# One-core graph attention kernel: peeling bits with fewer dependent VectorE steps, capping empty slots while own scores are added, and a reordered ending with more spare matmuls

## What is computed

```
h = x @ W
e = (h @ a1)[:, None] + (h @ a2)[None, :]
e = where(e > 0, e, 0.2 * e)
e = where(adj > 0, e, -9e15)
y = x + elu(softmax(e, axis=1) @ h)
out = (y - mean(y)) / sqrt(var(y) + 1e-5)
```

## Time and profile before

| | us |
|---|---|
| three timed runs | 715.48, 714.63, 712.79 (median 714.63) |
| the profiled execution, its own time | 716.63 |
| its span, first to last instruction | 714.8 |
| share of the span in which PE, DVE, ACT, POOL were busy | 78%, 67%, 73%, 63% |
| mean granted clock of PE, as a share of full speed | 0.874 |

### The profile page before, as it was taken

The page is one execution under the profiler, slowest core; times in us unless marked ns, Lnnn a source line. Parts: engine busy times, 40 slices in busy tenths (PEclk is TensorE's granted clock), DMA queues, the critical chain, the costliest instruction groups (busy, mean ns, idle before and its releaser), DMA issues.

```text
span 714.8 us, 11813 instructions
## 1 busy us (share of the span) xinstructions
PE 558.3 (78%) x3025; PEld 352.9 (49%) x3074; DVE 479.6 (67%) x2059; ACT 521.6 (73%) x416; POOL 447.1 (63%) x676
## 2 busy tenths in 40 slices
PE   0867887776979787777788778887787988887985
PEld 0323455453546554544555555554455555545564
DVE  2375577776585867677666667677666577675774
ACT  0847778787877887878788777878787788787601
POOL 2015367767575776677666766767667577677771
PEclk9979999988887989999999988899999688888976
DMA  9999999999999999999999999999999999999362
GB/s 352 328 416 429 426 424 426 426 423 425 425 427 429 426 426 428 427 427 426 427 425 427 431 425 426 428 427 427 428 426 428 431 425 426 426 427 423 128 182 73
DMA packets 34598, 285.57 MB, mean 399 GB/s; under 512 B 5528, under 2 KB 13872, under 8 KB 18064
## 3 DMA queue, kind: packets, MB, share of 16 engines
q1 hardware_dynamic: 29024, 276.83, 92.7%
q0 software_dynamic: 5120, 8.42, 3.3%
q10 hardware_dynamic: 432, 0.07, 0.1%
HBM read 283.18 MB, written 4.19 MB: 402 GB/s over the span
## 4 chain that ended last, share of the span: by engine, by line
DMA 64%; PE 16%; ACT 11%; issue 4%; DVE 2%; POOL 1%; SPq 1%; ACTq 0%; POOLq 0%; DVEq 0%
DMA adj_sb<-in_adj 62%; ACT adj_squared L603 10%; PE fold L718 8%; DMA a_sb<-in_L_gnn_a 2%; PE x_att_ps L771 1%; PE misc L748 1%; PE fold L714 1%; PE fold L830 1%; PE small L733 1%; PE small L757 1%; POOL edge_row L375 1%; SPq L413 1%; PE x_att_ps L774 0%; PE h_ps L798 0%; PE fold L785 0%
## 5 line engine op out<-in xcount | busy, mean ns | idle before, releaser
L603 ACT ACTIVATE adj_squared<-adj_sb 128x4096 bf16<-128x4096 int32 x128 | 462.5, 3614 | 105.6 <-DMA adj_sb<-in_adj 99.7
L718 PE MATMUL fold<-adj_sb,bit_ident 128*128 128x512 bf16 x993 | 302.9, 449 | 10.2 <-DMA adj_sb<-in_adj 4.8
L528 POOL DMA_INDIRECT nb<-in_x,index x160 | 165.9, 1037 | 90.3 <-issue 59.8
L718 PEld LDWEIGHTS fold<-adj_sb,bit_ident 128*128 128x128 bf16 x1024 | 110.8, 108 | 154.2 <-issue 68.1
L953 DVE MAX8 top_map<-fold 128x8 f32<-128x512 f32 x128 | 89.3, 699 | 70.7 <-PE fold L718 57.0
L714 PE MATMUL fold<-col_no,ident_bf 128*128 128x512 bf16 x112 | 47.8, 426 | 104.9 <-DMA adj_sb<-in_adj 90.9
L375 POOL TENSOR_SCALAR edge_row<-row_iota,edge_in 128x128 f32<-128x128 int32 x186 | 128.9, 707 | 0.0
L393 POOL TENSOR_TENSOR spread<-edge_row,edge_w 128x384 f32<-128x384 f32 x60 | 55.0, 935 | 74.6 <-DVE edge_w L1079 74.6
L508 POOL TENSOR_SCALAR empty_diag<-ident,counts 128x128 f32<-128x128 f32 x64 | 39.5, 623 | 64.3 <-DVE counts L989 33.5
L714 PEld LDWEIGHTS fold<-col_no,ident_bf 128*128 128x128 bf16 x128 | 16.4, 128 | 125.0 <-issue 86.8
L771 PEld LDWEIGHTS x_att_ps<-spread,nb 128*128 128x128 f32 x372 | 57.5, 221 | 8.0 <-issue 4.1
(11 more groups left out here) (139 smaller groups left out, 631.2 us busy)
## 6 DMA issues: line engine op xcount, KB each, us to landing
adj_sb<-in_adj SPq DMA_DIRECT2D x127, 2048.0 KB, 14.8
out<-x_sb SPq DMA_DIRECT2D x2, 1536.0 KB
nb<-in_x,index POOLq DMA_INDIRECT x160, 2.4
adj_sb<-in_adj SPq DMA_DIRECT2D x2, 1024.0 KB, 17.0
out<-x_sb SPq DMA_DIRECT2D x4, 128.0 KB
out<-x_sb SPq DMA_DIRECT2D x1, 384.0 KB
out<-x_sb SPq DMA_DIRECT2D x2, 64.0 KB
W_sb<-in_L_gnn_W ACTq DMA_DIRECT2D x1, 64.0 KB, 7.8
```

The source lines that it names most:

```text
L528: nc.gpsimd.indirect_dma_start(out=nb_of(j, g)[:, c, :], out_offset=None, in_=x[:, :], in_offset=bass.IndirectOffsetOnAxis(ap=index[:, g, ...
L603: nc.scalar.activation(adj_squared[:, h % 2, :], adj_sb[:, h % LOAD_SLOTS, :], ACT.Square, accum_out=half_sum[:, h:h + 1]).then_inc(square ...
L718: last = nc.tensor.matmul(fold[:, h % LOAD_SLOTS, :], bit_ident[:, b, :], adj_low[:, h % LOAD_SLOTS, b * FOLD:(b + 1) * FOLD, 0], start=Fa ...
```

## The change

Three things are edited.

**Peeling.** Before, `lists` took the codes apart one after another: subtract the column, mask the exponent (the leading bit), subtract it, mask the exponent again. Now a scaled copy of the numbers, larger by 2^8, is made first (`peel[:, 0, :]`), so that the leading bit can be masked with the column still in place, and the two masks that give `lead` are one instruction of twice the width, which keeps only the low bits of the exponent. There are eight instructions before the first `max` as before; seven of them were followed by a wait for their own end, now five are. A constant is set once at the start.

**Cap.** `scores` applied `cap` by an instruction of its own after the leaky slope. Now the row's own part is added and the cap applied in one instruction for each tile (two of 128 x 10), and the separate one (128 x 20) is gone.

**Ending.** On ACT `copy_sums(back2)` comes ahead of `exp_weights(back1)`. On PE two calls of `keep_warm` grow from 4 and 5 to 8 and 8 matmuls, and a `keep_warm(2)` is added behind `send_scores(final)`.

```diff
-    FIRST_EXP = 127 + 9
+    LIFT = 2.0 ** 8
+    KEPT_BITS = 0b00010111 << 23
+    FIRST_EXP = 16
     COL_0 = FOLD * (FIRST_EXP + BITS - 1) + HALF
-    NO_CODE = COL_0 - N - FOLD
+    NO_CODE = COL_0 - N
...
-                copy_sums(*back2)
                 exp_elu(*back2)
...
                 exp_elu(*back3)
+                copy_sums(*back2)
                 exp_weights(*back1)
...
-                keep_warm(4)
+                keep_warm(8)
                 send_shares(*back1)
-                keep_warm(5)
+                keep_warm(8)
                 send_scores(*final)
+                keep_warm(2)
                 sum_neighbours(*back1)
...
-                    v.after(nc.vector.tensor_scalar(top_int[:], top_map[:].rearrange("p q s -> p (q s)"),
-                                                    1.0 / UNIT, float(FOLD // 2), ALU.mult, ALU.add))
+                    maps = top_map[:].rearrange("p q s -> p (q s)")
+                    nc.vector.tensor_scalar(peel[:, 0, :], maps, LIFT / UNIT, LIFT * (FOLD // 2), ALU.mult, ALU.add)
+                    v.after(nc.vector.tensor_scalar(top_int[:], maps, 1.0 / UNIT, float(FOLD // 2), ALU.mult, ALU.add))
+                    nc.vector.tensor_tensor(top_lead[:], peel[:, 0, :].bitcast(i32),
+                                            exp_bits[:, 0:1].to_broadcast(flat), ALU.bitwise_and)
                     v.after(nc.vector.tensor_tensor(top_col[:], top_int[:], col_bits[:, 0:1].to_broadcast(flat),
                                                     ALU.bitwise_and))
-                    nc.vector.tensor_tensor(from_base[:], half_base[:].rearrange("p q s -> p (q s)"), top_col[:],
-                                            ALU.subtract)
-                    v.after(nc.vector.tensor_tensor(top_code[:], top_int[:], top_col[:], ALU.subtract))
-                    v.after(nc.vector.tensor_tensor(lead[:, 0, :], top_code[:].bitcast(i32),
-                                                    exp_bits[:, 0:1].to_broadcast(flat), ALU.bitwise_and))
-                    v.after(nc.vector.tensor_tensor(rest_code[:], top_code[:], lead[:, 0, :].bitcast(fp32),
+                    nc.vector.tensor_tensor(peel[:, 1, :], peel[:, 0, :], top_lead[:].bitcast(fp32), ALU.subtract)
+                    v.after(nc.vector.tensor_tensor(from_base[:], half_base[:].rearrange("p q s -> p (q s)"), top_col[:],
                                                     ALU.subtract))
-                    v.after(nc.vector.tensor_tensor(lead[:, 1, :], rest_code[:].bitcast(i32),
-                                                    exp_bits[:, 0:1].to_broadcast(flat), ALU.bitwise_and))
+                    v.after(nc.vector.tensor_tensor(
+                        lead[:].rearrange("p k s -> p (k s)"), peel[:].rearrange("p k s -> p (k s)").bitcast(i32),
+                        kept_bits[:, 0:1].to_broadcast([P, PEELS * 2 * PAIR * 8]), ALU.bitwise_and))
...
-                    mine = s_all[:, bass.ds(j * BODY + g * PAIR, PAIR)]
-                    v.after(nc.vector.tensor_tensor(score[:], t_row_ps, mine.unsqueeze(2).to_broadcast(slots),
-                                                    ALU.add))
+                    for t in range(PAIR):
+                        last = nc.vector.scalar_tensor_tensor(
+                            score[:, t, :], t_row_ps[:, t, :], s_all[:, bass.ds(j * BODY + g * PAIR + t, 1)],
+                            cap[:, g, t, :], ALU.add, ALU.min)
+                    v.after(last)
                     v.after(nc.vector.scalar_tensor_tensor(score_l[:], score[:], ALPHA, score[:],
                                                            ALU.mult, ALU.max))
-                    v.after(nc.vector.tensor_tensor(score_l[:], score_l[:], cap[:, g, :, :], ALU.min))
```

More of the change, by code:

```diff
@@ L120, in graph_attention @@
         exp_bits = sb("exp_bits", [P, 1], i32)
+        kept_bits = sb("kept_bits", [P, 1], i32)
         half_base = sb("half_base", [P, 2 * PAIR, 8], i32)
@@ L149, in graph_attention @@
         top_col = sb("top_col", [P, 2 * PAIR * 8], i32)
-        top_code = sb("top_code", [P, 2 * PAIR * 8], fp32)
-        rest_code = sb("rest_code", [P, 2 * PAIR * 8], fp32)
+        peel = sb("peel", [P, PEELS, 2 * PAIR * 8], fp32)
+        top_lead = sb("top_lead", [P, 2 * PAIR * 8], i32)
         from_base = sb("from_base", [P, 2 * PAIR * 8], fp32)
@@ L911, in _ @@
                 nc.vector.memset(exp_bits[:], EXP_BITS)
+                nc.vector.memset(kept_bits[:], KEPT_BITS)
                 nc.vector.memset(col_bits[:], FOLD - 1)
```

## The result

| | before | after |
|---|---|---|
| median of 9 timed runs, us | 715.28 (711.57 to 719.98) | 720.06 (718.39 to 722.79) |
| ratio after / before | | 1.0071, 95% interval 1.0046 to 1.0097 |
| the profiled execution, its own time | 716.63 | 722.79 |
| its span | 714.8 | 721.0 |
| last packet of adjacency ends (DMA records) | 670.2 | 679.3 |

The change costs 4.8 us by the medians: it is slower where faster was forecast, and 720.06 lies above the predicted range of 707.7 to 712.5. The last two lines say where, for the two profiled executions: the loop lost 9.1 us, and what follows it won back 2.9.

What follows compares the result with a forecast made beforehand. DMA bounds the loop to 664 us, then a PE, DVE, ACT, POOL chain, with PE at half clock. Gains of 4.9 and 0.95 make 5.85: 710.8 from the profile, 708.8 from the median; 709.6 taken, range 707.7 to 712.5.

Steps and rivals of the forecast that it cites:

- the loop to 664 unchanged: Loop, 60 to 664 us: DMA covers peeling and cap, so both are worth nothing there; without cover 8 us.
- a constant more at the start: Start of the kernel: the new constant's instruction lies behind the first transfers, so no cost was counted.
- the 5.85 us of all the others: Ending: 4.9 us to the final shares plus 0.95 us of DVE idle time, for an execution like the profiled one.
- the 0.06 for a slower kernel: Whole kernel: chance 0.06 that it is slower by 3.6 us.
- the half-clock products: Ending, PE: clock already down at `times_W(back2)`, nine more products cost 3.9 us on the path; 716.7 us, chance 0.06.
- The sum: Whole change: 5.85 us off the profiled 716.63 gives 710.8; 709.6 was taken as the forecast.
- The 4.9 us to the end of `send_shares(final)`: Ending, PE: at full clock the final shares are done at 696.7 instead of 701.61, 4.9 us sooner.
- the term of 0.95: Ending, DVE: its idle 0.96 us before the final group's first tile goes, worth 0.95 us.
- The first rival: Ending: timed runs lose less to the clock than the profiled one, leaving 3.85 us; 710.8 us, chance 0.22.
- The later fall: Ending, PE: the clock still falls, at about 693, and 3.2 of 5.85 us are gone; 712.0 us, chance 0.14.
- the gather: Ending, DVE: gathered rows land late for the final `t_slot`, up to 2.5 us of gain go; 711.3 us, chance 0.08.
- the small edits only: Ending: the reorder does not remove PE's idle time, only DVE's 0.25 us remain; 714.4 us, chance 0.05.

Runs made afterwards that it cites:

- e1: The changed kernel with 352 unused bytes ahead of `nb`, so that it starts at a multiple of 512 again; 710.96 us, ratio 0.9935.
- e3: The kernel before with the edits of the ending alone, `nb` where it was; 710.22 us, ratio 0.9930.
- e5: The kernel before with `nb` alone 32 bytes off its multiple of 512; 722.10 us, ratio 1.0089.
- e10: The kernel before with `nb` alone 256 bytes off its multiple of 512; 714.44 us, ratio 1.0005.
- e9: The kernel before with `nb` alone 128 bytes off its multiple of 512; 725.79 us, ratio 1.0123.
- e6: The kernel before with `nb` alone 64 bytes off its multiple of 512; 723.82 us, ratio 1.0102.

## Why the prediction was wrong

**The step that failed** is the one that put the loop at nothing: "the loop to 664 unchanged", and before it "In the loop both are worth nothing, since DMA covers them". The reading was right, the loop is bound by DMA and nothing computed in it can shorten it. The conclusion was not, for an edit can also change the DMA. The prediction knew of "a constant more at the start" and priced it by its instruction, which "lies behind the first transfers". Its 32 bytes, and the 128 of the wider temporaries, cost 9.1 us by pushing `nb` off a multiple of 256: the term that was put at nothing is larger than the 5.85 us of all the others. None of the rivals had it, and the 0.06 for a slower kernel rested on the half-clock products or on "a wait that I don't see". Where one resource is at a share of 1.01 for 600 us, 1.4% more time on each of its packets (615.4 to 624.1 ns) is worth more than the whole change to the ending.

With `nb` placed back the rest can be judged:

- **The sum.** Predicted 709.6 for the whole change; e1 has 710.96. Its profiled execution took 709.25, where the sum had 710.8 for one like the profile before; 1.2 of the 1.55 us between are luck, for its final `pick` ended 2.3 us behind the last packet and not 3.5 (see the last point of this list).
- **The ending.** The mechanism was right at each station: copy ahead of the exponential, `times_W` straight behind the scores, clock 1.00, products hidden by the wait for `share`. The 4.9 us to the end of `send_shares(final)` came too: from the end of the final `pick` it is 701.61 - 673.65 = 28.0 us before, and 22.9 in the changed kernel. The term of 5.85 us for an execution like the profiled one held: from the end of the final `pick` to the start of DVE's last instruction it is 711.09 - (672.37 + 1.28) = 37.4 us before, and 717.25 - (684.60 + 1.28) = 31.4 after, 6.1 us less. That only 2.9 us of it show in the table of the result is because the final `pick` itself ended 6.6 us behind the last packet, and 3.5 before. DVE before, then after:

```profile
672.37 1.28 DVE L953 MAX8 top_map<-fold 128x8 f32<-128x512 f32 x2
...
711.09 0.14 DVE L1138 CAST n_bad<-n_bad_f 1x1 int32<-1x1 f32 x1
```

```profile
684.60 1.28 DVE L960 MAX8 top_map<-fold 128x8 f32<-128x512 f32 x2
...
712.51 0.17 DVE L1111 TENSOR_SCALAR late_var<-mean_var 128x2 f32<-128x2 f32 x1
712.64 0.23 DVE L1126 TENSOR_SCALAR z_one<-z_exp 128x128 f32<-128x128 f32 x1
...
717.25 0.14 DVE L1146 CAST n_bad<-n_bad_f 1x1 int32<-1x1 f32 x1
```

DVE no longer idles before the first `finish_tile` (712.51 + 0.17 to 712.64, where the earlier trace rows had 0.96): the term of 0.95 as well.

- **The first rival**, that timed runs have less to give back, is partly borne out. e3 gives 5.0 us by its ratio, interval 3.1 to 7.0, which holds the 3.85 of the rival and the 5.85. Profiles show why a single one misleads. From the end of the final `pick` to the start of DVE's last instruction the old ending took 33.5 to 37.4 us in nine profiles, mean 36.1, and the new one 31.2 to 31.5 in five. The profile before was one of the longest of the nine, so the 5.85 us were the most that there was to win, and the mean of these profiles has 4.7. In e5, one of the shortest, the same 1.77 us of idle time was there and the clock fell behind it, but it was back at full between 698 and 699.
- **Peeling:** 0.18 us a group, as predicted (1.71 to 1.53). **Cap:** the start of the scores to `row_max` is 657.97 - 657.37 = 0.60 us now and 0.63 before (607.71 to 608.34); 0.03, at the low side of 0 to 0.11 and less than the 0.07 taken. From the first of the two new instructions to the one behind them it is 657.75 - 657.37 = 0.38, where spacings of 0.11 and 0.22 would give 0.33. The timed runs cannot resolve either edit. DVE before, then after:

```profile
607.71 0.16 DVE L1056 TENSOR_TENSOR score<-misc,s_all 128x20 f32<-128x20 f32 x1
...
608.34 0.17 DVE L1061 TENSOR_REDUCE row_max<-score_l 128x2 f32<-128x20 f32 x1
```

```profile
657.37 0.35 DVE L1063 SCALAR_TENSOR_TENSOR score<-misc,s_all,cap 128x10 f32<-128x10 f32 x2
657.75 0.18 DVE L1067 SCALAR_TENSOR_TENSOR score_l<-score 128x20 f32<-128x20 f32 x1
657.97 0.17 DVE L1069 TENSOR_REDUCE row_max<-score_l 128x2 f32<-128x20 f32 x1
```

The measurement that the Trainium skill tells on its page "VectorE: DVE Perf Modes", section "The DRAIN you can't avoid", by which a chain takes as long with a wait behind each operation as with one at the end, is not borne out for these operations of 32 elements a row: an unwaited pair starts 0.11 us apart and a waited one 0.22 in the changed kernel too.

- **The later fall, the half-clock products, the gather, the small edits only:** none came. The clock is 1.00 from 688 to 704, and the final group's `t_slot` does not wait.
- **What the sum did not have:** the time from the last packet to the end of the final `pick`, which only the two small edits touch. It follows PE's clock in the last 8 us of the loads. Where that was 1.00, the `pick` ended 2.2 to 2.3 us behind the last packet (seven profiles); at 0.84 to 0.90, 3.5 to 3.9 (five, the kernel before among them); at 0.50, 6.3 to 6.6 (four, the changed kernel among them). The changed kernel, then e1, columns as in the first fence of the result:

```profile
671.30:679.30 8.00, 7.78 (x33) 6.30 (x33) 3.92 (x22) 2.56 (x2) 1.54 (x4) 0.50 0.47 196
```

```profile
662.20:670.20 8.00, 7.87 (x56) 5.83 (x56) 5.99 (x30) 6.45 (x6) 5.53 (x13) 1.00 0.49 203
```

PE is as busy in both and gets through 33 matmuls in one and 56 in the other. The 4.3 us between these two (6.6 against 2.3) are nearly all of the difference between 41.7 us behind the last packet in the changed kernel and 37.2 in e1. Old and new endings stand in each of the three groups, so the edits do not decide it, and why the clock was low in some executions stays open: no run was made for it.

## What to carry to other kernels

Where transfers bound a stretch, an edit that touches no transfer can still change them: any tensor added, widened or dropped moves the buffers behind it. Before pricing an edit, list where the buffers of the transfers start, before and after; put the destination of gathered rows at a multiple of 256 bytes and that of large loads at a multiple of 512 (for these nothing in between was tried), and pin it there with a pad. When a DMA share stays at its limit while GB/s fall, look at the duration of single packets, and at what other queue runs where they are long.

## What the runs showed of the hardware

- **Start of a gather's destination.** Rows of 512 bytes from indirect transfers went into a buffer 32, 64, 128 or 160 bytes past a multiple of 512: 15% of the 16,384-byte packets on the loads' queue, nearly all of them beside a gather, then take some 677 ns instead of 615, and the loop 9 us more. 256 past it costs nothing. The gather's queue moves 8.42 of 285.57 MB, 2.9% of the bytes, and its own packets of 4,096 bytes hardly lengthen (171 to 173 ns); its neighbours pay. The Trainium skill, page "DMA: Bandwidth & Descriptors", section "How a descriptor splits into AXI transactions", says that a descriptor which starts at a multiple of 256 is cut into transactions of 256 bytes, and that a transaction which reads must start at such a multiple. By that, and this is an estimate, a row of 512 bytes that starts between two multiples takes three transactions instead of two. The multiple agrees with e10 against e9. The page says it of reads; here it is the place of the destination that was changed, and why large packets on another queue are the ones delayed, no run here shows.
- **Start of a large load's destination.** 128 bytes past a multiple of 512: 615.4 ns a packet; at the multiple 612.2, and the last packet ends 4.2 us sooner (670.2 to 666.0). `adj_sb` at a multiple of 256 that is none of 512 was not tried.
- **The two together.** A displaced `nb` costs 9.1 us with `adj_sb` displaced and 5.7 us with it in place. This stays open.
- **The clock.** With the same code, a stretch of the ending differs from one execution to the next by as much as the edits gained. e5 and e6 have the same ending: from the last packet on e5 took 39.6 us and e6 47.5. From 697 to 713 the mean clock was 0.86 in e5 and 0.58 in e6. The new ending took this out behind the final `pick` (31.2 to 31.5 us in five profiles), but not ahead of it.
